# Node degrees by counting equal places in each edge tile, and half-precision one-hots of up to eight counting steps in one instruction

## The reference

```python
agg = segment_sum(x[src], dst)
deg = segment_sum(ones, dst)
mean = agg / maximum(deg, 1)[:, None]
return mean @ Wl + bl + x @ Wr
```

## Time and profile before

| | |
|---|---|
| median of 3 runs | 5190.62 us (5187.66 to 5204.27) |
| the profiled execution, its own time | 5186.65 us |
| its span | 5184.8 us |
| TensorE busy (matmuls) | 3908.8 us, 75% |
| VectorE busy | 2480.8 us, 48% |
| GpSimd busy | 3527.4 us, 68% |
| ScalarE busy | 700.4 us, 14% |
| layer 0's bodies | from 145 to 2449 us |

### The profile page before, as it was taken

The page is one execution under the profiler, slowest core; times in us unless marked ns, Lnnn a source line. Parts: engine busy times, 40 slices in busy tenths (PEclk is TensorE's granted clock), DMA queues, the critical chain, the costliest instruction groups (busy, mean ns, idle before and its releaser), DMA issues.

```text
span 5184.8 us, 72837 instructions
## 1 busy us (share of the span) xinstructions
PE 3908.8 (75%) x17697; PEld 2653.5 (51%) x17702; DVE 2480.8 (48%) x8026; ACT 700.4 (14%) x1817; POOL 3527.4 (68%) x3567
## 2 busy tenths in 40 slices
PE   3345777777767877444989999999988687888886
PEld 1233544444444544444866666666657444444446
DVE  4547888888888887443522222222216122222222
ACT  3000112222223332000410000000001100000002
POOL 1656777776667777775157777777764577777774
PEclk6556676666666555555989999999989888888887
DMA  5111233433344445213377676776765988888886
GB/s 165 46 37 42 97 98 121 144 141 141 143 146 160 171 161 193 71 52 69 116 236 204 202 209 201 207 205 201 210 204 174 266 217 216 218 217 217 217 206 211
DMA packets 781611, 848.91 MB, mean 164 GB/s; under 512 B 69895, under 2 KB 676505, under 8 KB 774394
## 3 DMA queue, kind: packets, MB, share of 16 engines
q1 hardware_dynamic: 654570, 560.41, 35.8%
q0 software_dynamic: 123712, 285.69, 19.5%
q10 hardware_dynamic: 3152, 1.06, 0.1%
HBM read 634.91 MB, written 211.98 MB: 163 GB/s over the span
## 4 chain that ended last, share of the span: by engine, by line
PE 36%; DVE 21%; issue 17%; POOL 11%; DMA 7%; DVEq 7%; SPq 1%; ACT 0%; POOLq 0%; ACTq 0%
PE ps L869 13%; PE ps L999 12%; POOL ring L640 10%; DVE area L1300 8%; DMA ring<-table,idx_now 5%; DVE big L1184 5%; DVE degree_hot L1159 3%; DVEq L1187 3%; PE ps L894 2%; DVE area L1159 2%; PE ps L1041 2%; PE ps L1026 2%; DVEq L1184 1%; DVEq L1300 1%; PE ps L876 1%
## 5 line engine op out<-in xcount | busy, mean ns | idle before, releaser
L640 POOL DMA_INDIRECT ring<-table,idx_now x3376 | 3373.3, 999 | 1319.8 <-issue 1059.1
L869 PE MATMUL ps<-onehot,ring 128*128 128x32 f32 x8712 | 1323.5, 309 | 696.3 <-DVE degree_hot L1159 425.9
L869 PEld LDWEIGHTS ps<-onehot,ring 128*128 128x128 f32 x8712 | 1329.6, 233 | 997.6 <-issue 993.9
L1184 DVE TENSOR_TENSOR big<-big,ps 128x32 f32 (+1 forms) x3376 | 666.9, 198 | 2338.0 <-PE ps L869 1598.5
L999 PE MATMUL ps<-area 128*128 128x512 f32 (+1 forms) x2744 | 1391.7, 653 | 24.8 <-DMA area<-table 23.9
L894 PE MATMUL ps<-area 128*128 128x392 f16 x2208 | 726.1, 512 | 342.3 <-DVE area L1300 340.3
L999 PEld LDWEIGHTS ps<-area 128*128 128x128 f32 x2744 | 558.6, 216 | 570.8 <-issue 546.3
L894 PEld LDWEIGHTS ps<-area 128*128 128x128 f16 x2208 | 289.8, 140 | 677.4 <-issue 568.6
L744 ACT ACTIVATE idx_now<-idx_all 128x5 int32 (+3 forms) x716 | 147.4, 207 | 3293.4 <-PE ps L869 2157.2
L1300 DVE TENSOR_SCALAR area<-iota_code,area 128x392 f16<-128x392 f16 x2208 | 565.0, 325 | 0.0
L757 ACT ACTIVATE big<-ps 128x392 f32<-128x392 f32 x736 | 364.9, 497 | 750.0 <-PE ps L894 748.4
(11 more groups left out here) (125 smaller groups left out, 1178.6 us busy)
## 6 DMA issues: line engine op xcount, KB each, us to landing
edge_count<-big SPq DMA_DIRECT2D x46, 3136.0 KB
area<-edge_count SPq DMA_DIRECT2D x98, 1472.0 KB
area<-edge_count SPq DMA_DIRECT2D x98, 960.0 KB, 6.1
ring<-table,idx_now POOLq DMA_INDIRECT x3376
area<-table SPq DMA_DIRECT2D x98, 256.0 KB, 6.7
ring<-input SPq DMA_DIRECT2D x98, 256.0 KB, 2.7
input<-ring SPq DMA_DIRECT2D x48, 512.0 KB, 3.8
area<-table SPq DMA_DIRECT2D x98, 128.0 KB
```

The source lines that it names most:

```text
L640: pool.indirect_dma_start(out=ring[:, g * n + j, 0:width], out_offset=None, in_=table[layer][:, :], in_offset=bass.IndirectOffsetOnAxis(ap ...
L869: last = nc.tensor.matmul(to[:, m * W:(m + 1) * W], ring[:, k, m * P:(m + 1) * P], onehot[:, k, :], start=True, stop=True)
L1184: V.tensor_tensor(sums, sums, step, ALU.add).then_inc(s_acc[layer], 1)
```

## The change

Degrees: the per-tile one-hots and their 1580 matmuls go. In their place, once for each of the 32 places w of a window, `window_degrees` marks on VectorE which of the 1664x128 edges have place w (one compare over 1664), sums the marks for each of the 13 chunks of tiles (a reduction over 1664), makes a one-hot of each tile's node w within its block (one compare of 13x128) and 13 block one-hots of 98 multiplied by the count. TensorE then has 13 matmuls a window place. These run in the 16 plain bodies, two places a body, ahead of parts 0 and 2. `window_nodes` (5 operations over 416 elements) runs once in body 0. Two of the four edge tables are no longer transposed.

Counting: codes and values are half precision; up to eight steps are made by one compare for the 128-wide and one for the 392-wide one-hots, stored with the steps innermost. TensorE then reads both operands of a counting matmul with 16 bytes between neighbouring elements. A constant of 392x8 half-precision numbers (`codes`) is written by GpSimd ahead of the step tables.

```diff
+        stats = sb("stats", [P, 2 * CHUNKS, 6])
+        rstd = sb("rstd", [P, BLOCKS])
+        rel_f = area[:, 0:STEPS]
-        low_hot = area[...].bitcast(f16).rearrange("p (s n) -> p s n", n=P)
+        low_hot = area[...].bitcast(f16).rearrange("p (b n s) -> p b n s", n=P, s=LANES)
+        code_hot = area[...].bitcast(f16).rearrange("p (b n s) -> p b n s", n=CODES, s=LANES)
...
+            body(at, window_node(at))
+            with eng.Fori(at + 1, BODIES[0] - 1) as i:
+                body(i, window_node(i))
+            body(BODIES[0] - 1, window_node(BODIES[0] - 1))
...
+            pool.iota(codes, [[1, CODES], [0, LANES]], base=0, channel_multiplier=0, **f).then_inc(s_const, 1)
...
-            for k, nat in enumerate((src_f, rel_f, loc_f, blk_f)):
+            for k, nat in enumerate((src_f, rel_f)):
...
-            pe.wait_ge(s_edges, 4)
+            pe.wait_ge(s_edges, 2)
...
-                if layer == 0:
-                    pe.wait_ge(s_degree_hot, i * PARTS + (g + 1))
-                if layer == 0:
-                    for j in range(n):
...
-                        last = nc.tensor.matmul(degree_ps, hot[:, P:P + BLOCKS], hot[:, 0:P], start=first, stop=end,
...
-                        nc.tensor.matmul(ps[:, 4 + k % 4, 0:CODES], low_hot[:, slot % SLOTS, :], code_hot[:, slot % SLOTS, :],
+                        half_slots, lane = slot % SLOTS // LANES, slot % LANES
+                        nc.tensor.matmul(ps[:, 4 + k % 4, 0:CODES], low_hot[:, half_slots, :, lane], code_hot[:, half_slots, :, lane],
...
+            def sum_degrees(w, half):
+                pe.wait_ge(s_degree_hot, w * 3 + 3)
+                hots = degree_hot[half]
+                for c in range(KCH):
+                    nc.tensor.matmul(degree_ps, hots[:, c, P:P + BLOCKS], hots[:, c, 0:P],
...
+            def window_degrees(w, half):
+                hots = degree_hot[half]
+                dve.wait_ge(s_count_step, COUNT_STEPS)
+                V.tensor_scalar(here, rel_f, iota_row[:, ds(w, 1)], None, ALU.is_equal).then_inc(s_degree_hot, 1)
+                one_hots(hots[:, :, 0:P], iota_code[:, 0:P], window_loc[:, ds(w * KCH, KCH)])
+                dve.wait_ge(s_degree_hot, w * 3 + 1)
+                V.reduce_sum(wrong[:, 0, :], here.rearrange("p (c e) -> p c e", c=KCH), mybir.AxisListType.X).then_inc(s_degree_hot, 1)
+                dve.wait_ge(s_degree_hot, w * 3 + 2)
+                for c in range(KCH):
+                    ins = V.tensor_scalar(hots[:, c, P:P + BLOCKS], iota_code[:, 0:BLOCKS], window_blk[:, ds(w * KCH + c, 1)],
+                                          wrong[:, 0, c:c + 1], ALU.is_equal, ALU.mult)
+                ins.then_inc(s_degree_hot, 1)
...
-                    if layer == 0 and not (last and g == PARTS - 1):
-                        degree_hots(i, g)
...
-                    one_hots(low_hot[:, at:at + count, :], iota_code[:, 0:P], low_all[:, ds(step + done, count)])
-                    for c in range(count):
-                        V.tensor_scalar(code_hot[:, at + c, :], iota_code[:, :], code_all[:, ds(step + (done + c), 1)], None,
-                                        ALU.is_equal).then_inc(s_count_hot, 1)
+                    for hots, w, values in ((low_hot, P, low_all), (code_hot, CODES, code_all)):
+                        ins = V.tensor_tensor(hots[:, half_slots, :, lane:lane + count], codes[:, 0:w, 0:count],
+                                              values[:, ds(step + done, count)].rearrange("p (a s) -> p a s", a=1).to_broadcast([P, w, count]),
+                                              ALU.is_equal)
+                    ins.then_inc(s_count_hot, count)
```

More of the change, by code:

```diff
@@ L366, in if_irregular, with first_bodies @@
             return eng.If(nc.values_load(outside[0:1, 0:1], engines=[eng.engine], min_val=0, max_val=1 << 24) > 0)
-        def first_bodies(eng, body, counting):
+        def first_bodies(eng, body, counting, degrees=lambda w, half: None):
             for i in range(TABLE_BODIES):
@@ L394, in first_bodies, with window_node @@
                     at += b - a
-            with eng.Fori(at, BODIES[0] - 1) as i:
-                body(i, lambda g: None)
-            body(BODIES[0] - 1, lambda g: None)
+            assert 2 * (BODIES[0] - at) == W
+            def window_node(i):
+                return lambda g: degrees(i * 2 + (g // 2 - 2 * at), g // 2) if g % 2 == 0 else None
+            body(at, window_node(at))
+            with eng.Fori(at + 1, BODIES[0] - 1) as i:
+                body(i, window_node(i))
+            body(BODIES[0] - 1, window_node(BODIES[0] - 1))
         def dense_bodies(eng, layer, body):
@@ L1143, in _ @@
             layer_norm(0)
[L1144 removed]
+            for k, to in enumerate((idx_all[:, :], rel_all[:, :])):
                 dve.wait_ge(s_edgeT, k + 1)
@@ L1190, in nodes_of, with window_nodes @@
                 return values
-            def degree_hots(i, g):
-                n = PER_PART[0]
-                i, g = (i + 1, 0) if g == PARTS - 1 else (i, g + 1)
-                some = ds(i * PER_BODY[0] + g * n, n)
-                here = degree_hot[:, g % 2 * n:(g % 2 + 1) * n, :]
-                one_hots(here[:, :, 0:P], iota_code[:, 0:P], loc_all[:, some])
-                one_hots(here[:, :, P:P + BLOCKS], iota_code[:, 0:BLOCKS], blk_all[:, some]).then_inc(s_degree_hot, 1)
+            def window_nodes():
+                by_place = lambda a: a.rearrange("p (w c) -> p w c", c=KCH)
+                link(V.tensor_tensor(by_place(window_loc), iota_row[:, 0:W].rearrange("p (w a) -> p w a", a=1).to_broadcast([P, W, KCH]),
+                                     first_node[:, :].rearrange("p (a c) -> p a c", a=1).to_broadcast([P, W, KCH]), ALU.add))
+                link(V.tensor_copy(window_i.bitcast(i32), window_loc))
+                link(V.tensor_scalar(window_blk_i.bitcast(i32), window_i.bitcast(i32), P.bit_length() - 1, None, ALU.arith_shift_right))
+                link(V.tensor_copy(window_blk, window_blk_i.bitcast(i32)))
+                link(V.scalar_tensor_tensor(out=window_loc, in0=window_blk, scalar=-float(P), in1=window_loc, op0=ALU.mult, op1=ALU.add))
+            def window_degrees(w, half):
[10 more added lines that the diff above has]
+                ins.then_inc(s_degree_hot, 1)
             def add_parts(layer, i, counting=lambda g: None, last=False):
@@ L1309, in body_0 @@
                         tables_for_picks()
+                        window_nodes()
                     if i == 1:
```

40 lines of the change are left out of this document (20 added, 20 removed).

## The result

The changed kernel takes **5509.11 us** (median of four runs, 5508.03 to 5511.2) where the kernel before takes 5189.14 beside it: a ratio of 1.061, interval 1.059 to 1.063. Slower by 320 us, where I had forecast 4958 us; it is the first rival, TensorE's strided operands, and nearer to its upper end (twice the dense time, 5527) than to the middle that I had given it (5418). Behind every median of this text the executions lie within 0.5% of one another, but for one of 6932 us among the four of the repeated 8-byte kernel (4974.2 us without it), which has no trace and stays unexplained.

The account below looks back on a forecast made before the run. The bound was taken to change by stage, VectorE in the 12-step counting bodies, with GpSimd's gathers as floor. Terms 5 - 66 - 141 - 33 - 21 + 27 = -229 from 5186.65 gave 4958 us; range 4875 to 5265, the forecast's own 4875 to 5057.

Parts of the forecast that it names:

- the first rival: Counting matmuls: operands 16 bytes apart slow TensorE, 0.328 us to twice that each; priced at 5418 us, slower; chance 0.13.
- TensorE's is 12 matmuls in 4.10 us: 12-step counting parts: matmul time kept as before; with 2.1 for the sum and 0.3 handing over, 6.5 us at worst.
- break-even (0.50 us): Strided-operand rival: time of one counting matmul at which the change neither gains nor loses.
- the terms outside the counting: Start, table bodies and plain bodies of layer 0: 5 - 66 + 27, or -34 us.
- Rows 9: Profile rows of two 32-element VectorE additions: 216 ns with an input 24 bytes apart, 193 ns with 8; read as 1.7 times.
- the gain in the table bodies: First bodies of layer 0, degree one-hots and matmuls gone: 245 instead of 311 us, -66 (-74 to -51).
- the loss in the plain bodies: Last 16 bodies of layer 0, window degrees lock out gathers: 428 against 401 us, +27 (+8 to +39).
- the compares at 3.9 us a part: 12-step counting parts: four half-precision compares, 6240 elements at 0.62 ns, take 3.9 us where 4.84 stood.
- the start: Before the first block: `codes` costs 11 us, earlier transposes give -5.7; net +5 us (-2 to +10).
- I take 0.2 us a part: Counting bodies: GpSimd's lock-out by VectorE's compares, added to its 6.24 us a part.
- the lock-out rival: Counting bodies: new compares lock GpSimd out for 0.27 to 0.52 of their time; 5195 us, no change; chance 0.08.
- the 6.4, 6.55 and 6.4 forecast: Time a part in the 14, 24 and 16 counting bodies, in us, for -33, -141 and -21 us.

Follow-up runs that it names:

- 8-byte kernel: Changed kernel with up to four steps in a compare instead of eight, operand neighbours 8 bytes apart, everything computed: 4977.78 us (0.959); repeated, 4974.84 us.
- the run with both dense: Changed kernel with both operands of the counting matmuls read from a dense constant of the same shape, counts left out: 5164.54 us (0.995).
- the two best kernels: The 8-byte kernel, 4977.78 us, and the one with pairs, 4984.07 us.
- pairs: Changed kernel with one-hots stored codes innermost, each value kept twice side by side, up to four steps a compare, everything computed: 4984.07 us (0.961).

## Why the prediction was wrong

*The step that failed* is "TensorE's is 12 matmuls in 4.10 us": the price of a counting matmul was taken over unchanged for operands with 16 bytes between elements. It is 0.697 us, not 0.34, and this makes the difference of sign: with dense operands the changed kernel takes 5165 us and not 5509. 0.712 - 0.329 = 0.383 us on 2208 matmuls is 845 us more of TensorE's busy time, of which 489 + 988 + 482 - 1592 = 367 us show, the rest having filled TensorE's waits. The rival held the mechanism, its break-even (0.50 us) and its reason (an element to a line); its upper end of twice the dense time gave 5527, 18 us off. That closeness is luck: the price was 0.697 us where 0.656 stood, which adds 91 us, and what stood around the matmuls was (1959 - 2208 x 0.697)/216 = 1.94 us a part where 2.4 stood, which takes 98 off; the terms outside the counting took another 12. What was wrong was the weight, 0.13. My reason against it was that a slower clock might hide the limit. It does not: the limit is 1.78 ns a column, above the 0.83 ns (0.327 us for 392) of a dense one at 1.2 GHz. Rows 9 would have given that price: 0.72 ns on 1.04 makes 1.76 ns an element for VectorE, and 392 x 1.76 is 0.69 us. I used it as a ratio where it could have been a time; one instruction of another engine at another distance, so the match may be luck.

*Right, with their sizes:* the gain in the table bodies (-74 for -66), where GpSimd's wait for indices fell from 67.0 to 1.5 us; the loss in the plain bodies (+31 for +27); the compares at 3.9 us a part (0.69 + 1.79 + 0.42 + 0.97 = 3.87). *Off:* the start, -3 for +5, with `codes` at 5.68 us for 11, the midpoint of two figures of which the lower, 5.8, was right.

*Second, hidden behind the first:* "I take 0.2 us a part" for the lock-out (gathers held up by VectorE). In the run with both dense the gathers take 5 x (1.205 - 0.945) = 1.3 us a part longer than undisturbed ones. That is the lock-out rival: 5195 us, measured 5165; parts of 7.8, 7.5 and 7.3 us, measured 7.66, 7.33 and 7.1. The reason for the 0.2 was "The single-tensor compares that I blame for most of it go", and the trace of the kernel before already speaks against it:

```profile
1337.56 1.98 DVE L1300 TENSOR_SCALAR area<-iota_code,area 128x392 f16<-128x392 f16 x8
1337.99 0.94 POOL L640 DMA_INDIRECT ring<-table,idx_now  x1 [1.07 <-ACT idx_now L744]
...
1342.54 1.22 DVE L1159 TENSOR_TENSOR area<-iota_code,area 128x1024 f16<-128x1024 f16 x1
1343.16 1.40 POOL L640 DMA_INDIRECT ring<-table,idx_now  x1 [0.30 <-issue]
```

The first gather runs beside single-tensor compares of L1300, which last 0.25 us each, and loses nothing; the second starts beside a two-tensor compare of 1024 elements and ends 0.8 us behind it. In the 24 bodies of that kernel the gathers lose 81 us in all over 0.944 us each: 71 in those that start beside a two-tensor half-precision compare of L1159, 7 in the 140 that start beside one of L1300. The plain bodies were no evidence against it, as their compares last 0.82 us at most. So with TensorE put right and nothing else the change would have been worth half a per cent. The forecast of 4958 us holds only for the kernel with compares of four steps, where both prices are small: 4978 us, with parts of 6.6, 6.6 and 6.5 us for the 6.4, 6.55 and 6.4 forecast.

## What to carry to other kernels

Before a layout is turned to suit the engine that writes it, price the engine that reads it: a moving operand of TensorE whose neighbours lie 16 bytes apart ran at 1.78 ns a column here, and at 8 bytes at half of that, whichever level of the clock was granted. Measure how long an instruction of VectorE holds GpSimd's gathers before making it longer; the two best kernels here make compares of at most 1568 elements, where the changed one makes 3136 in one. And where a row of another engine shows a penalty, carry it over as a time as well as a ratio.

## What the runs showed of the hardware

- TensorE's half-precision moving operand, 392 columns, from start to start: 0.348 us at 8 bytes, at 1.2 and at 2.4 GHz alike; 0.697 at 16 bytes and 0.707 at 32, seen at 1.2 GHz only; dense 0.327 at 1.2 GHz and 0.166 at 2.4. One read of VectorE at 24 bytes fits the same 1.8 ns.
- With TensorE busy all the time on such matmuls the granted clock stayed at 0.50; with dense or 8-byte ones in the same bodies it was higher. In the 24 bodies: changed kernel, busy 988 of 988 us, 0.50; 8 bytes, 545 of 632 at 0.71; pairs, 440 of 644 at 0.75; both dense, 438 of 735 at 0.73.
- A gather that starts while a two-tensor operation of VectorE with both tensors in SBUF runs ends 0.82 us behind it, at the rate of 1.04 ns an element (the compare of 1024 elements above) and at twice that rate. Only a gather that starts within 0.02 us of the operation's start escapes it: ten such gathers beside compares of 3136 elements in the run with both dense took 0.94 us, and one that started 0.027 us behind took 2.57. One beside `accumulate` (an operand in PSUM) or beside a reduction keeps its 0.94 us: in the kernel before, from 171.32 us, beside the reduction that runs from 170.24 to 172.13. The Trainium skill ("SBUF — State Buffer", Who interferes with whom) says that an operation with two SBUF inputs contends with GpSimd instructions that read SBUF, but infers that tensor_tensor leaves GpSimd's making of descriptors alone; the indirect gathers of this kernel, which read their indices from SBUF, end behind it, and the measurement decides.
- Rows of two half-precision numbers, one of them a repeated value, run at the faster of the two rates (0.97 us for 1568 elements in the kernel with pairs).
- Not so rows with an odd number of half-precision steps. The few such compares in the changed kernel, 392 rows of 1, 3, 5 and 7, took 2.14, 2.01, 1.93 and 1.91 us, where rows of 2 took 0.85 and rows of 8 took 1.79. Such rows also start or end at an odd element of the 16 bytes; the two were not told apart.
